# A GNN kernel on one core: setup reordered, three rounds written out, gather lists spread with three ring slots

## What is computed

```python
def _L0_gnn_ref(node_features, edge_features, src, dst, W, b):
    agg_src = jax.ops.segment_sum(node_features[src], dst, num_segments=N_NODES)
    agg_edge = jax.ops.segment_sum(edge_features, dst, num_segments=N_NODES)
    h = jnp.concatenate([node_features, agg_src, agg_edge], axis=1)
    return jax.nn.relu(h @ W.T + b)

def _sage_conv(x_src, x_dst, src, dst, n_dst, W_l, b_l, W_r):
    agg = jax.ops.segment_sum(x_src[src], dst, num_segments=n_dst)
    deg = jax.ops.segment_sum(jnp.ones((src.shape[0],)), dst, num_segments=n_dst)
    agg = agg / jnp.maximum(deg, 1.0)[:, None]
    return agg @ W_l + b_l + x_dst @ W_r

h = relu(layernorm(x));  x = x + _L0_gnn_ref(h, edge_attr_128, src, dst, W, b)
h = relu(layernorm(x))
h = relu(_sage_conv(h, h, src, dst, ...)); x = x + relu(_sage_conv(h, h, src, dst, ...))
```

## Time and profile before

| | us |
|---|---|
| median of 3 runs (lowest, highest) | 1514.26 (1512.93, 1514.72) |
| the profiled execution, its own time | 1511.41 |
| its span from first to last instruction | 1509.6 |
| busy: TensorE, VectorE, ScalarE, GpSimd | 1384.2, 825.2, 486.0, 658.6 |
| mean granted TensorE clock, share of full | 0.977 |
| chain that ended last, by engine | TensorE 55%, GpSimd 25%, issue 10%, VectorE 5% |

### The profile page before, as it was taken

The page is one execution under the profiler, slowest core; times in us unless marked ns, Lnnn a source line. Parts: engine busy times, 40 slices in busy tenths (PEclk is TensorE's granted clock), DMA queues, the critical chain, the costliest instruction groups (busy, mean ns, idle before and its releaser), DMA issues.

```text
span 1509.6 us, 36666 instructions
## 1 busy us (share of the span) xinstructions
PE 1384.2 (92%) x12165; PEld 1243.5 (82%) x12166; DVE 825.2 (55%) x1839; ACT 486.0 (32%) x1388; POOL 658.6 (44%) x768
## 2 busy tenths in 40 slices
PE   4586999999999999989999988999999899998966
PEld 4455999999999999988888876888888688887855
DVE  6777998888888888853455454422222222221111
ACT  2351123455788888852222322211111010000000
POOL 4301000111121112237177777274777737577772
PEclk9998999999999999999999999999999999999988
DMA  6007678888889898876354655565656656666562
GB/s 173 25 6 198 201 223 233 238 243 252 263 266 265 265 271 266 261 257 189 136 181 150 205 174 161 166 195 165 203 194 207 182 157 211 200 218 200 184 159 62
DMA packets 284676, 294.52 MB, mean 195 GB/s; under 512 B 19414, under 2 KB 250017, under 8 KB 284625
## 3 DMA queue, kind: packets, MB, share of 16 engines
q1 hardware_dynamic: 235541, 213.75, 45.6%
q0 software_dynamic: 26016, 69.24, 16.1%
q10 hardware_dynamic: 23067, 10.89, 2.5%
HBM read 245.70 MB, written 48.11 MB: 195 GB/s over the span
## 4 chain that ended last, share of the span: by engine, by line
PE 55%; POOL 25%; issue 10%; DVE 5%; DMA 2%; ACT 2%; ACTq 0%; DVEq 0%; POOLq 0%
POOL shared L826 25%; PE edge_banks L1008 19%; PE edge_banks L1044 16%; PE banks L982 11%; PE edge_banks L1004 3%; DMA shared<-g_rows,list_src 2%; PE edge_banks L1075 1%; PE banks L919 1%; PE banks L1062 1%; ACT shared L1217 1%; PE edge_banks L851 1%; DVE edge_t L1378 1%; ACT banks L1212 0%; DVE g_even L1448 0%; DVE shared L1329 0%
## 5 line engine op out<-in xcount | busy, mean ns | idle before, releaser
L826 POOL DMA_INDIRECT shared<-g_rows,list_src x555 | 540.8, 974 | 272.2 <-issue 169.9
L1044 PE MATMUL edge_banks<-g_even,shared 128*128 128x257 f16 (+1 forms) x3822 | 446.6, 274 | 5.5 <-DMA shared<-counts 4.6
L1044 PEld LDWEIGHTS edge_banks<-g_even,shared 128*128 128x128 fp8e3 x3822 | 373.6, 98 | 64.7 <-issue 4.8
L1008 PE MATMUL edge_banks<-shared 128*128 128x128 f32 x2744 | 339.9, 276 | 0.0
L1008 PEld LDWEIGHTS edge_banks<-shared 128*128 128x128 f32 x2744 | 323.6, 193 | 0.0
L806 POOL DMA_DIRECT2D counts<-shared x156 | 76.5, 491 | 460.4 <-ACT shared L1217 442.0
L1596 DVE SCALAR_TENSOR_TENSOR shared<-edge_banks,shared,own 128x128 f32<-128x128 f32 x98 | 34.4, 351 | 384.9 <-PE edge_banks L1044 335.1
L1044 PE MATMUL edge_banks<-shared 128*128 128x256 f16 x1911 | 225.8, 272 | 0.9 <-DVE own L1578 0.9
L1522 DVE TENSOR_TENSOR shared<-iota,shared 128x3528 f16<-128x3528 f16 x98 | 195.4, 1994 | 47.2 <-PE banks L982 46.8
L1217 ACT ACTIVATE shared<-banks 128x392 uint16<-128x392 f32 x312 | 152.3, 488 | 187.6 <-PE banks L982 178.5
L1044 PEld LDWEIGHTS edge_banks<-shared 128*128 128x128 fp8e3 x1911 | 185.3, 97 | 31.4 <-DVE own L1578 1.2
(11 more groups left out here) (276 smaller groups left out, 1012.1 us busy)
## 6 DMA issues: line engine op xcount, KB each, us to landing
shared<-in_edge_attr SPq DMA_DIRECT2D x195, 512.0 KB, 4.6
shared<-counts SPq DMA_DIRECT2D x117, 784.0 KB
counts<-shared POOLq DMA_DIRECT2D x156, 196.0 KB, 4.0
shared<-g_rows,list_src POOLq DMA_INDIRECT x555
shared<-hot_rows SPq DMA_DIRECT2D x20, 304.0 KB
g_rows<-g_even SPq DMA_DIRECT2D x1, 3136.0 KB, 15.1
g_rows<-shared ACTq DMA_DIRECT2D x49, 64.0 KB
g_rows<-g_even ACTq DMA_DIRECT2D x49, 64.0 KB
```

What stands on the lines that cost most here:

```text
L826: pool.indirect_dma_start(ring_g[k % 2][:, t, 0:2 * D], None, g_rows[r], bass.IndirectOffsetOnAxis(ap=list_src[:, at + t:at + t + 1], axis ...
L1008: mm = pe.matmul(edge_wide[bank][:, :, at], ring[:, bank * GROUP_TILES + j, :], hot_dst[u][:, k, (j - 1) * SPREAD:j * SPREAD].unsqueeze(1) ...
L1044: mm = pe.matmul(acc[s][:, 0:wide], stream8[slot][:, order[h], :], G[r % 2][:, order[h], 0:wide], start=h == 0, stop=h == BLOCKS - 1, skip ...
```

## The change

1. Marks: 7 groups of 112 and one of 128 columns, each product takes 128 columns from its group's start (912 marks).
2. Constants: GpSimd's memset of 2428 elements covers 4.
3. VectorE's order in the setup: counts of the marks read as soon as they are there, both halves of the statistics ahead of the steps, the bounds ahead of the ends, `pick` behind the step tables.
4. The list starts move from before the layer norm to its turn t == 2 on TensorE and pair b == 4 on VectorE (the tables and checks from b == 4 to b == 8), the product of the checks to t == 6 and its reading to b == 40.
5. GpSimd clears hot_dst and edge_t once the field is ready, before go; TensorE zeroes its banks before go.
6. Rounds: all 49 positions written out, on every engine. Lists at positions 6, 11, 15, 20, 25, 29, 34, 38, 43, 47. Three ring slots. The four stream slots are counted over dense blocks only.

The core of the diff (renamed calls without `it` left out):

```diff
+LIST_AT = (6, 11, 15, 20, 25, 29, 34, 38, 43, 47)
+RING = 3
...
-    MARKS = (PER + 1) * HOLDERS
+    MARKS = PER * HOLDERS + P
...
-        def whole_round(eng, one, between=None):
-            one(0, 0)
-            if between is not None:
-                between()
-            for i in range(1, FIRST):
-                one(i, 0)
-            with eng.Fori(0, LOOPS) as it:
-                for i in range(FIRST, FIRST + LOOP):
-                    one(i, it)
-            one(FIRST + LOOP, LOOPS - 1)
...
+        DENSE_AT = [i for i in range(BLOCKS) if i not in LIST_AT]
+        def is_listed(i):
+            return i in LIST_AT
+        def place_of(i):
+            return DENSE + list_of(LIST_AT.index(i)) if is_listed(i) else DENSE_AT.index(i)
+        def done_at(n):
+            return n + 5
...
@@ SyncE, rounds
+                    def one(i):
+                        n = number(r, i)
+                        if i > 0 and r == 0 and is_listed(i - 1):
+                            k = LIST_AT.index(i - 1)
+                            sp.wait_ge(R["list_hot"], k + 1)
+                            sp.dma_start(hot_rows[k], list_hot_u8.rearrange("p t d -> p (t d)")).then_inc(S["hot_stored"], 16)
                         if is_listed(i):
+                            if r > 0:
+                                k = LIST_AT.index(i)
+                                last = number(r, LIST_AT[k - 1]) if k > 0 else number(r - 1, LIST_AT[-1])
+                                sp.wait_ge(R["summed"], done_at(max(last, n - 4)))
+                                sp.dma_start(list_hot_u8.rearrange("p t d -> p (t d)"), hot_rows[k]).then_inc(S["hot_landed"], 16)
                             return
+                        g = stream_use(r, i)
+                        if g >= 4:
+                            sp.wait_ge(R["summed"], done_at(number_of_use(g - 4)))
+                        sp.dma_start(stream[g % 4], counts[place_of(i)]).then_inc(stream_landed[g % 4], 16)
...
@@ GpSimd
-            pool.memset(place(22068, 2428), 0.0)
+            pool.memset(place(22068, 4), 0.0)
...
+            pool.wait_ge(S["field_ready"], 1)
+            for u in range(2):
+                pool.memset(hot_dst[u][:, :, GROUP_TILES * SPREAD:GROUP_HOT], 0.0).then_inc(S["edge_cleared"], 1)
+            pool.memset(edge_t[:, :], 0.0).then_inc(S["edge_cleared"], 1)
             pool.wait_ge(S["go_ready"], 1)
...
                     for k in range(LISTED):
-                        done = r * BLOCKS + FIRST + 4 * k if k >= 2 else r * BLOCKS + 4 * k - 1
-                        if k >= 2 or r > 0:
-                            pool.wait_ge(R["summed"], done)
+                        use = list_use(r, k)
+                        if use >= RING:
+                            old = use - RING
+                            pool.wait_ge(R["summed"], done_at(number(old // LISTED, LIST_AT[old % LISTED])))
                         for t in range(LIST_TILES[k % 2]):
...
@@ TensorE
-                    mm = pe.matmul(flat[0][0:HOLDERS, j:j + 1], cmp16[:, b, j * HOLDERS:(j + 1) * HOLDERS], ones16[:, 0:1],
+                    mm = pe.matmul(flat[0][:, j:j + 1], cmp16[:, b, j * HOLDERS:j * HOLDERS + P], ones16[:, 0:1],
...
                 if t > 0:
                     dense(t - 1)
+                if t == 2:
+                    pe.wait_ge(S["tables_ready"], 1)
+                    pe.wait_ge(S["pick_ready"], 1)
+                    pe.wait_ge(S["rows_iota"], 1)
+                    for c in range(LBLK):
...
+                    mm.then_inc(S["list_up"], 1)
...
+                if t == 6:
+                    pe.wait_ge(S["viol_ready"], 1)
+                    pe.matmul(flat[0][0:1, 80:85], ones[:, 0:1], viol, start=True, stop=True).then_inc(S["viol_up"], 1)
...
+            pe.wait_ge(S["field_taken"], 2)
+            pe.wait_ge(S["cell_ready"], 1)
+            for c in range(BANKS):
+                pe.matmul(banks[:, c, :], zeros16[:, 0:P], zeros16[:, 0:1].broadcast_to([P, 512]), start=True, stop=True)
+            pe.wait_ge(S["list_tables"], 2)
+            for c in range(BANKS):
+                mm = pe.matmul(flat[c], zeros16[:, 0:P], zeros16[:, 0:1].broadcast_to([P, 512]), start=True, stop=True)
+            mm.then_inc(S["zeroed"], 2 * BANKS)
             pe.wait_ge(S["go_ready"], 1)
...
-                    if r == 0:
-                        whole_round(pe, one, lambda: pe.wait_ge(S["zeroed"], 2 * BANKS + 2 * NDUO))
-                    else:
-                        whole_round(pe, one)
+                    for i in range(BLOCKS):
+                        if r == 0 and i == 1:
+                            pe.wait_ge(S["zeroed"], 2 * BANKS + 2 * NDUO)
+                        one(i)
...
@@ VectorE, loop over pairs
                 if b == 4:
+                    dve.wait_ge(S["list_up"], 1)
+                    dve.tensor_copy(list_base, flat[0][:, 76:76 + LBLK])
+                    dve.tensor_copy(dense_edges, flat[0][0:1, 72:73])
+                    dve.tensor_scalar(list_at, flat[0][:, 72:72 + LBLK], 0.0, float(E + P - LEFT), ALU.max, ALU.min).then_inc(S["list_starts"], 1)
+                if b == 40:
+                    dve.wait_ge(S["viol_up"], 1)
+                    link(dve.tensor_reduce(guard[:, 0:1], flat[0][0:1, 80:85], AX_X, ALU.add))
+                    link(dve.tensor_scalar(flags[0:1, 0:1], guard[:, 0:1], 0.0, None, ALU.is_equal))
+                if b == 8:
                     dve.tensor_copy(iota_a, iota_f[:, 0:LO_A].unsqueeze(2).broadcast_to([P, LO_A, STEPS_ROW]))
...
-                        if r == 0 and FIRST <= i < FIRST + LOOP and (i - FIRST) % 4 == 0:
+                        if r == 0 and is_listed(i + 3):
```

More of the change, by code:

```diff
@@ L611, in to_turn, with before, after, number @@
                 return (1,) if r > 0 else ()
[L612 to L626, removed]
-        def whole_round(eng, one, between=None):
-            one(0, 0)
-            if between is not None:
-                between()
-            for i in range(1, FIRST):
-                one(i, 0)
-            with eng.Fori(0, LOOPS) as it:
-                for i in range(FIRST, FIRST + LOOP):
-                    one(i, it)
-            one(FIRST + LOOP, LOOPS - 1)
[L639 to L643, removed]
-        def uses(r, i, it):
-            earlier = sum(PER_SLOT[(slot_of(r, i) - q) % 4] for q in range(r))
-            return it * (16 * LOOP // 4) + 16 * (earlier + i // 4 + 1)
+            return () if is_listed(i) else (2, 1) if is_listed(i - 1) else (1,)
+        def before(i, back):
+            return place_of((i - back) % BLOCKS)
+        def after(i):
+            return place_of((i + 1) % BLOCKS)
+        def number(r, i):
+            return r * BLOCKS + i
+        def stream_use(r, i):
+            return r * DENSE + DENSE_AT.index(i)
+        def number_of_use(g):
+            return number(g // DENSE, DENSE_AT[g % DENSE])
+        def list_use(r, k):
+            return r * LISTED + k
+        def tiles_landed(r, k):
+            return sum(LIST_TILES[q % LISTED % 2] for q in range(list_use(r, k) % RING, list_use(r, k) + 1, RING))
+        def done_at(n):
+            return n + 5
         def block_at(b):
@@ L796, in build @@
             def build():
-                for u in range(2):
-                    pool.memset(hot_dst[u][:, :, GROUP_TILES * SPREAD:GROUP_HOT], 0.0).then_inc(S["edge_cleared"], 1)
-                pool.memset(edge_t[:, :], 0.0).then_inc(S["edge_cleared"], 1)
                 def store(b, s):
@@ L1247, in high @@
                             o = (s + back) % 2
-                            at = block_at(before(i, it, back) if back else place_of(i, it))
+                            at = block_at(before(i, back))
                             act.wait_ge(R["g_up"], n + 1 - back)
@@ L1280, in one @@
                                 store(1)
-                    whole_round(act, one)
-                    b = place_of(FIRST + LOOP, LOOPS - 1)
+                    for i in range(BLOCKS):
+                        one(i)
+                    b = place_of(BLOCKS - 1)
                     act.wait_ge(R["g_done"], (r + 1) * BLOCKS + 2)
```

288 lines of the change are left out of this document (118 added, 170 removed).

## The result

The kernel after takes 1467.4 us (median of 4 runs, 1463.7 to 1471.9), the kernel before beside it 1514.5 us (1512.9 to 1515.8): ratio 0.969, interval [0.967, 0.971]. The forecast was 1480.1 us with a range from 1474: right in sign, 13 us short in size.

What follows compares the result with a forecast made beforehand. GpSimd's gather issuing, trailing TensorE after waits for ring slots, was taken to bound the rounds; TensorE the build. Setup -3.4 and rounds -12.4, -9.0, -9.4 summed to -34.2 us off the median: 1480.1 us, range 1474 to 1488.

Steps and rivals of the forecast that it cites:

- Rounds 1 and 2: Rounds, spread lists and three slots: 9.0 us go in round 1, 9.4 in round 2, which GpSimd's issuing bounds.
- Round 0: First round, spread lists and three slots: TensorE's waits for gathers vanish, 12.4 us go.
- nothing is gained or lost there: Rounds: writing them out in full removes register arithmetic and adds code, with no effect on time.
- (a): Setup, shrinking GpSimd's memset from 2428 elements to 4 lets VectorE's first cast finish earlier: -2.0 us.
- (b): Setup, mark products with 128 columns take 41 ns instead of 95 and keep up with the compares: -5.1 us.
- (c): Setup, layer norm's products no longer wait for lists and bounds, so TensorE's transposes start earlier: -5.0 us.
- (d): Setup, list products moved inside the layer norm hold TensorE 7.55 us plus 0.8 of pipeline refill: +8.3 us.
- (e): Setup, TensorE's zeroing products go ahead of the go, so VectorE no longer idles for them: -3.4 us.
- (f): Setup, GpSimd's 6400-element memset moves beside VectorE's table work and holds up the int32 shift: +3.8 us.
- A: Rival, setup: GpSimd's moved memset holds nothing up, so its cost is 0 and the time 1476.3 us; chance 0.18.
- B: Rival, rounds: gathers land later and undo round 1's 9.0 us gain, giving 1489.1 us; chance 0.15.
- C: Rival, rounds: fetching the written-out code stalls TensorE, 1531 us at 1 us for each of 51 packets; chance 0.03.

Runs made afterwards that it cites:

- the control: Kernel after plus one max-with-0 register operation before each ScalarE and TensorE build wait on a loaded value; 2032.6 us beside 2043.6 for the kernel before.
- the kernel with the early clear: Against the control, GpSimd zeroes the edge table once layer 0's last dense block is taken, before the field is ready; 1473.1 us, ratio 0.9731.

## Why the prediction was wrong in size

**Rounds 1 and 2: right.** The waits went, and the stages are shorter by 9.0 and 9.5 us. GpSimd issues round 2 from 1212.58 to 1442.71 us without a break, 230.1 us, and the last list starts 233.4 us after its first gather (234 forecast). TensorE's pauses are fewer than forecast: 5.2 and 5.9 us at positions 15 and 38, 0.9 at 29 and none at 47.

**Round 0: the failed step is "nothing is gained or lost there", on writing out the rounds.** The waits did vanish (12.4 us), and 8.0 us came on top. I had taken the absence of a cost from the earlier trace rows, a stretch of dense blocks in round 2. For later rounds it holds: in round 1 a period takes 20.39 us looped and 20.40 written out, (1185.75 - 1022.53) / 8 in the kernel with old positions and three slots. In round 0 it does not. The cost stood in the period I used myself, 22.29 us, as a part of the pace of TensorE: three dense blocks of 6.23 us and a list of 2.3 us make 21.0, and I never asked what the other 1.3 us were. 0.77 of it went with the loops, 0.59 with VectorE's and 0.11 to 0.15 with ScalarE's. Nine periods lie between the first and the last list, so that is 9 x 0.77 = 6.9 us. The other 1.1 us lie ahead of the first list: 0.3 in the three dense blocks that were looped (transpositions 6.45 and 6.29 us apart instead of 6.23), and 0.8 in the first 24 products of the round, which took 4.76 us (675.64 to 680.40) before and 3.94 (670.58 to 674.52) after. There the clock rose earlier, which no part of the change was meant to do (with old positions and three slots they took 4.32); this 0.8 us is luck.

**Setup.** (a), (b) and (c) together: TensorE's first transposes moved from 65.64 to 52.94 us, -12.7 against -12.1. By rows, (a) is -2.3 (the first compare starts at 12.32 instead of 14.63 us), (b) -5.1 (the mark products end at 17.60 instead of 25.00), and (c) the other -5.3. (d) is the mis-sized term, 3.1 of the 4.0 us: the distance from the first transposes to the end of the dense products grew by 5.2 us, not 8.3. I took the 7.55 us of the products where they stood before; inside the layer norm they take 4.1 us (61.31 to 65.39). Those that come ahead take 223 ns at a granted clock of 0.50, those inside 116 ns at 1.00; TensorE had by then been at work on transposes and dense products from 52.94 us on. The other 1.1 us of the 5.2 do not come apart cleanly. The first sixteen dense products are done 8.5 us after the first transpose (7.5 before), the more of them at a clock of 0.50. Behind the list products the clock fell to 0.50 again, and the next eight dense products took 3.37 us, where eight take 2.28 at the full clock. The kernel before in turn lost about as much behind its pause for the index tables, where eight took 3.49 us. The window view of the kernel before shows 1.00 at the list products, but its clock record begins only at 69.0 us, and its products took 224 ns, like those at 0.50. I read a default as a measurement. (e) came to -3.3 against -3.4 (from the end of the dense products to the build 18.0 us before and 18.2 after, of which (f) adds 3.4). (f) came to +3.4 against +3.8: the shift waits until GpSimd's memset has ended.

**The rivals.** A fell: the shift was held, by one memset, from its start to the memset's end. That by itself fits the lock of one instruction that the Trainium skill describes (SBUF — State Buffer, Who interferes with whom); the earlier trace rows speak against it, and so does a cast in the setup of the kernel after, which spans the end of one and the whole of three more GpSimd instructions, the last of them ending at 7.95 us:

```profile
5.80 2.64 DVE L1324 CAST shared<-shared 128x912 f16<-128x912 int32 x1
```

B fell: no list of round 1 waited longer than 0.3 us. C fell: the instruction queue moved 61 packets instead of 27, and TensorE shows no gap for them in the kernel after (on the two starved chips it did, but the looped kernel before was slowed there as much). The trace of the kernel after agrees with the Trainium skill (Runtime: NRT & Kernel Launch, Instruction fetch mechanics), by which crossing a block of code is mostly hidden. The build took 2.3 us longer, in small waits spread over it; no cause was found.

## To carry to other kernels

A pace read from a trace holds costs too: take it apart into its instructions before it is used as the floor, above all at the short steps, where the helpers' latency shows. Where one engine trails by a fixed amount a round, more slots and earlier positions are two ways to the same end; one is enough, and savings elsewhere count only behind it. A step that is moved changes its price when the clock at its new place is another one, and it can change the clock of what stands behind it. A row of one round says nothing about another round in which the helpers have more to do.

## What the runs showed of the hardware

- On two chips TensorE stood without a releaser for some 400 us of the rounds. In the control, its waits of the rounds (total, times, longest) and its instruction queue (packets, MB, share of 16 engines):

```profile
PE edge_banks L1038 <- issue: 338.6, 289, 2.9
PE banks L1050 <- issue: 46.0, 10, 16.0
...
q8 instruction: 61, 1.00, 0.2%
```

 In these stretches single products were executed 0.7 or 1.4 us apart, the clock fell to 0.50, and the 61 packets of the instruction queue took about 1 us each (0.2% of 16 x 2032 us), as in the kernel after. The kernel before, looped, lost about as much (2043.6 us against 1512.6), and its trace on such a chip was not taken. The build, a small loop, lost nothing: it took 555.7 us there and 555.8 us in the kernel with the early clear on a good chip. The cause is open.
- One register operation ahead of each of the 704 waits that go by a register, on TensorE and ScalarE together, cost the build 9 to 13 us, a quarter to a third of the 39 us that the change gained in the rounds.
- The same products of one column took 223 ns at a granted clock of 0.50 and 116 ns at 1.00; 4.1 us of them came ahead of a fall of the clock from 1.00 to 0.50.
- VectorE's one-input operation on whole words, started 1.9 us into GpSimd's memset of 5.44 us, was held until the memset's end (3.69 us instead of 0.29); a two-input one of 2.02 us was not held at all.
